# Two-layer token-routing kernel: shared rows added to the output by accumulating transfers, the route mask on ScalarE, raw route weights, traces summed in pairs

## The reference, cut to what matters

```
# conditioning of one sequence (D = 8 decay rates)
ctx    = ema(x, tau_ctx)
gated  = x * sigmoid([x, ctx] @ Wg.T + bg)
mod    = 0.5 + sigmoid(gelu(x @ Wn1.T + bn1) @ Wn2.T + bn2)        # one column for each d
traces = [ema(gated * mod[:, d], tau_raws[d]) for d in range(8)]
temporal = sum_d softmax(blend)[d] * traces[d]
out    = (gelu(x @ Wsoma.T + bsoma) * sigmoid(temporal @ Wtemp.T + btemp)) @ Wout.T
z      = (out - mean) / sqrt(var + 1e-5) * gamma + beta
# expert layer over all 4096 tokens (64 experts, 8 for each token, at most 128 tokens for each expert)
w      = top8(softmax(z @ router.T)); w = w / sum(w)
routed = sum over the 8 experts of  w_e * ((silu(z @ Wgate_e) * (z @ Wup_e)) @ Wdown_e)
shared = (silu(z @ gate) * (z @ up)) @ ws_down
x      = x + routed + shared
```

## Time and profile before

| | |
|---|---|
| median of 3 runs | 1121.03 us (1117.95 to 1122.76) |
| profiled execution, its own time | 1116.69 us |
| its span, from the first to the last instruction | 1114.9 us |
| busy share of the span | PE 86%, DVE 67%, POOL 60%, ACT 41% |
| granted TensorE clock, mean | 0.929 of full |

### The profile page before, as it was taken

How to read it: one execution, slowest core, us unless ns; L and a number is a source line. 1 busy time by engine, 2 the same in 40 slices (tenths; PEclk the granted TensorE clock), 3 DMA queues, 4 the chain that set the end, 5 groups by cost and what they waited for, 6 DMA issues and landing times.

```text
span 1114.9 us, 14811 instructions
## 1 busy us (share of the span) xinstructions
PE 954.6 (86%) x4524; PEld 668.5 (60%) x4524; DVE 743.1 (67%) x1522; ACT 461.2 (41%) x835; POOL 664.1 (60%) x496
## 2 busy tenths in 40 slices
PE   4968999999999999987379899988586899999960
PEld 2533698899989998863144555544353565556640
DVE  3648566667666766524779999999955786777620
ACT  1330444554455545533455665666421232222320
POOL 2113444555455544407999999999931477777870
PEclk9989999999999999988689999999887799999995
DMA  5869234444354432223212752335168599997557
GB/s 174 281 231 352 58 76 118 90 87 99 76 122 90 92 88 39 30 85 76 96 66 70 240 157 86 91 118 182 44 229 274 143 270 256 257 262 150 91 75 157
DMA packets 89782, 155.46 MB, mean 139 GB/s; under 512 B 12072, under 2 KB 70128, under 8 KB 86576
## 3 DMA queue, kind: packets, MB, share of 16 engines
q1 hardware_dynamic: 48112, 91.27, 25.2%
q0 software_dynamic: 25104, 39.86, 20.6%
q10 hardware_dynamic: 16496, 23.49, 6.2%
HBM read 119.56 MB, written 43.42 MB: 146 GB/s over the span
## 4 chain that ended last, share of the span: by engine, by line
POOL 13%; PE 10%; issue 10%; DMA 9%; DVE 4%; ACT 2%; POOLq 2%; DVEq 1%; ACTq 0%; SPq 0%
DMA odd_rows<-ys,slots 5%; POOL wide L635 4%; PE bank L1662 4%; POOL wide L643 3%; DMA xg<-z_rows,slots 2%; POOL xg L721 2%; POOL out L728 2%; POOL odd_rows L728 2%; DVE wide L1271 1%; PE bank L1739 1%; PE bank L1729 1%; PE bank L1722 1%; ACT zrow L945 1%; DMA z_rows<-zrow 1%; ACT wide L895 1%
## 5 line engine op out<-in xcount | busy, mean ns | idle before, releaser
L635 POOL TENSOR_TENSOR wide<-wide 128x1024 f32<-128x1024 f32 x64 | 156.6, 2461 | 30.8 <-issue 30.6
L1271 DVE TENSOR_TENSOR_SCAN wide<-bank,wide 128x512 f32<-128x512 f32 x128 | 149.3, 1209 | 22.8 <-POOL wide L635 22.6
L871 ACT ACTIVATE h_raw<-bank,b 128x512 f32<-128x512 f32 x128 | 88.1, 689 | 168.1 <-PE bank L1635 165.7
L1208 DVE TENSOR_TENSOR h_lo<-h_raw,h_hi 128x512 fp32r<-128x512 f32 x128 | 87.3, 692 | 91.8 <-ACT h_hi L875 91.8
L1650 PE MATMUL bank<-w_hi,h_hi 128*128 128x256 f32 x512 | 144.4, 282 | 0.1
L1650 PE MATMUL bank<-w_lo,h_hi 128*128 128x256 f32 x512 | 142.1, 278 | 0.0
L1650 PE MATMUL bank<-w_hi,h_lo 128*128 128x256 f32 x512 | 142.0, 277 | 0.0
L609 POOL DMA_INDIRECT x_rows<-ob,put x64 | 110.3, 1723 | 28.3 <-issue 16.0
L643 POOL TENSOR_TENSOR wide<-wide 128x1024 f32<-128x1024 f32 x46 | 108.5, 2359 | 11.9 <-issue 8.1
L895 ACT ACTIVATE wide<-wide,blend 128x512 f32<-128x512 f32 x128 | 84.2, 715 | 59.3 <-POOL wide L635 55.5
L1635 PE MATMUL bank<-ex_hi,w_hi 128*128 128x512 f32 x256 | 99.5, 389 | 2.4 <-issue 2.4
(11 more groups left out here) (239 smaller groups left out, 2041.3 us busy)
## 6 DMA issues: line engine op xcount, KB each, us to landing
wide<-in_mwp SPq DMA_DIRECT2D x40, 512.0 KB, 4.5
wide<-m_rows SPq DMA_DIRECT2D x16, 1024.0 KB, 4.9
w1s<-in_fW SPq DMA_DIRECT2D x8, 1024.0 KB, 5.4
w2s<-in_fW SPq DMA_DIRECT2D x8, 1024.0 KB, 5.3
own<-in_mwp SPq DMA_DIRECT2D x15, 512.0 KB, 4.4
z_rows<-zrow SPq DMA_DIRECT2D x8, 640.0 KB, 7.4
head<-in_mwp SPq DMA_DIRECT2D x9, 512.0 KB, 4.5
xT<-in_xT ACTq DMA_DIRECT2D x8, 512.0 KB, 4.2
```

The costliest lines, as they stand in the source:

```text
L635: G.tensor_tensor(drive[n % DRIVES], gb[d % 2], md[d // HD][:, d % HD, :].unsqueeze(1).to_broadcast([P, CT, S]), ALU.mult).then_inc(c_u, 1)
L871: A.activation(h1_raw[f % 4][:, :], bank[:, 2 + f % 4, :], ACT.Gelu_apprx_tanh, bias=b1_0[:, bass.ds(e, 1), f]).then_inc(b_h, 1)
L1208: V.tensor_tensor(h1_lo[:, f, :], h1_raw[f % 4][:, :], h1_hi[:, f, :].bitcast(F32), ALU.subtract).then_inc(b_lo, 1)
L1271: o = V.tensor_tensor_scan(dst[:, c, :], decay[:, d:d + 1].to_broadcast([P, S]), drive[(D * b + d) % DRIVES][:, c, :], 0.0, ALU.mult, ALU.add)
```

## The change

Five edits, all from the conditioning on:

- The base of the result is built in `out` itself: x is copied there, layer 0 adds its rows there, and the conditioning loads its sequences from there. `x1_rows`, `row_in`, `row_store` and `finish` are gone. ACT halves the shared rows from PSUM into `ost` (`share_out`), and POOL issues a transfer that adds `ost` to `out` (`rows_add`).
- The 0/1 mask of sequences 0 to 6 is made by ACT in two instructions, Sign and Relu, straight into `mask_all` (`chosen_out`). The last sequence keeps the comparison on DVE, writing into `mask_all`.
- `zrow` holds the raw products of exponential and mask, and the inverse sum in column 320 (rows are 324 numbers long, 320 before); the expert stage multiplies the two single columns.
- Traces 3 and 4, and traces 5 and 6, are added to one another by DVE (`pair_traces`); POOL adds five sums a sequence (d = 1, 2, 4, 6, 7), DVE adds no single trace to `acc` except the last two of the last sequence.
- The two preparations for the power in `rstd_of` are ACT's (`moments`).

```diff
+        PAIRED = (4, 6)
+        SUMS = tuple(d for d in range(1, D) if d + 1 not in PAIRED)
...
 POOL
             def rstd_of(q):
-                pool.wait_ge(c_mv, level(q))
+                pool.wait_ge(c_mw, level(q))
                 pool.wait_ge(c_no, level(q - 1, TT))
-                G.tensor_scalar(veps1[:, :], mv1[:, :, 1], 4 * EPS, None, ALU.add)
-                G.tensor_scalar(shift1[:, :], mv1[:, :, 0], -1.0, None, ALU.mult)
-                pool.drain()
                 G.tensor_tensor(rstd1[:, :], veps1[:, :], mhalf[:, :], ALU.pow)
...
+            def rows_add(q):
+                pool.wait_ge(c_fin, level(q))
+                pool.dma_start(out[q * S:(q + 1) * S, :].rearrange("(t p) c -> p t c", p=P), ost[:, :, :],
+                               accum_op=ALU.add).then_inc(c_ost, 16)
...
             for e in range(ROWS):
                 e_gather(e)
 
-            pool.wait_ge(c_ost, level(B - 1, 16))
+            rows_add(B - 1)
+            wait_moved(pool, c_ost, B - 1, 16)
...
 ACT
+            def moments(q):
+                act.wait_ge(c_mv, level(q))
+                act.wait_ge(c_no, level(q - 1, TT))
+                A.activation(veps1[:, :], mv1[:, :, 1], ACT.Copy, bias=4 * EPS)
+                A.activation(shift1[:, :], mv1[:, :, 0], ACT.Copy, scale=-1.0).then_inc(c_mw, 1)
...
+            def chosen_out(q):
+                act.wait_ge(c_top, level(q))
+                A.activation(rep[:, :, :], rep[:, :, :], ACT.Sign, bias=far[:, :], scale=-1.0)
+                act.drain()
+                A.activation(mask_all[:, :, q * TT:(q + 1) * TT].rearrange("p e t -> p t e"), rep[:, :, :], ACT.Relu).then_inc(c_ma, 1)
...
+            def share_out(q):
+                act.wait_ge(c_dm, level(q))
+                wait_moved(act, c_ost, q - 1, 16)
+                A.activation(ost[:, :, :], rows4(4), ACT.Copy, scale=0.5).then_inc(c_fin, 1)
...
 DVE
+            def pair_traces(b, d):
+                n = (D - 1) * b + d - 1
+                dve.drain()
+                V.tensor_tensor(trace[n % TRACES], trace[n % TRACES], trace[(n - 1) % TRACES], ALU.add).then_inc(c_pair, 1)
+                dve.drain()
...
             def route_weights(q):
                 dve.wait_ge(c_ex, level(q))
                 dve.wait_ge(c_zst, level(q - 1, 16))
-                V.tensor_tensor(mask[:, :, :], mask[:, :, :], ex[:, :, :], ALU.mult)
+                if q < B - 1:
+                    dve.wait_ge(c_ma, level(q))
+                V.tensor_tensor(zrow[:, :, H:H + E1], ex[:, :, :], chosen(q), ALU.mult)
                 dve.drain()
-                V.tensor_reduce(wsum[:, :], mask[:, :, :], AX.X, ALU.add)
+                V.tensor_reduce(wsum[:, :], zrow[:, :, H:H + E1], AX.X, ALU.add)
                 dve.drain()
-                V.reciprocal(wsum[:, :], wsum[:, :])
-                dve.drain()
-                V.tensor_tensor(zrow[:, :, H:ZW], mask[:, :, :], wsum[:, :].unsqueeze(2).to_broadcast([P, TT, E1]),
-                                ALU.mult).then_inc(c_zr, 1)
+                V.reciprocal(zrow[:, :, H + E1], wsum[:, :]).then_inc(c_zr, 1)
-
-            def finish(q):
-                dve.wait_ge(c_dm, level(q))
-                dve.wait_ge(c_xr, level(q, 16))
-                dve.wait_ge(c_ost, level(q - 1, 16))
-                V.scalar_tensor_tensor(ost[:, :, :], rows4(4), 0.5, xr[:, :, :], ALU.mult, ALU.add).then_inc(c_fin, 1)
```

More of the change, by code:

```diff
@@ L222, in build @@
         neg = sb("neg", [P, TT, E1])
-        mask = sb("mask", [P, TT, E1])
+        far = sb("far", [P, 1])
         ex = sb("ex", [P, TT, E1])
@@ L418, in c_load @@
                 sp.wait_ge(c_Tm, level(n - 2))
-                sp.dma_start(x1t[n % 2], x1_rows[n * S:(n + 1) * S, :].rearrange("(t p) c -> p t c", p=P)).then_inc(c_in[n % 2], 16)
+                sp.dma_start(x1t[n % 2], out[n * S:(n + 1) * S, :].rearrange("(t p) c -> p t c", p=P)).then_inc(c_in[n % 2], 16)
             def e_load(e):
@@ L608, in b_put_rows @@
                 p = r & 1
-                G.indirect_dma_start(x1_rows[:, :], bass.IndirectOffsetOnAxis(ap=put[p][:, j:j + 1], axis=0),
+                G.indirect_dma_start(out[:, :], bass.IndirectOffsetOnAxis(ap=put[p][:, j:j + 1], axis=0),
                                      ob[p][:, j, :], None, compute_op=ALU.add).then_inc(b_put[p], 16)
@@ L663, in step @@
                     drive_of(b - 1, 7)
-                if on(b - 1):
-                    add_trace(b - 1, 5)
                 if ahead(b):
                     drive_of(b, 0)
+                if on(b - 3):
+                    rows_add(b - 3)
                 if ahead(b):
@@ L798, in _ @@
             a_store(B - 1)
-            act.dma_start(x1_rows.rearrange("(a r) c -> a (r c)", a=P), x_rows.rearrange("(a r) c -> a (r c)", a=P)).then_inc(x1_set, 16)
+            act.dma_start(out[0:TOK, :].rearrange("(a r) c -> a (r c)", a=P), x_rows.rearrange("(a r) c -> a (r c)", a=P)).then_inc(x1_set, 16)
             act.wait_ge(zeros_set, 1)
@@ L976, in step @@
                     shared_out(B - 2)
+                    moments(B - 1)
                     normalise(B - 1)
+                    share_out(B - 2)
                     return
@@ L1011, in step @@
                     weighted(b, 7)
+                if on(b - 1):
+                    moments(b - 1)
                 if ahead(b + 1):
                     wg_out(b + 1)
+                if on(b - 2):
+                    share_out(b - 2)
                 if on(b - 1):
@@ L1025, in last_step @@
                 shared_out(B - 1)
+                share_out(B - 1)
             def front_only():
@@ L1267, in scan_unit @@
                     n = (D - 1) * b + d - 1
-                    dve.wait_ge(c_add, level(n - TRACES))
+                    old, of = divmod(n - TRACES, D - 1)
+                    if of + 1 in SUMS and old >= 0:
+                        dve.wait_ge(c_add, added(old, of + 1))
                     dst = trace[n % TRACES]
@@ L1275, in add_trace @@
             def add_trace(b, d):
-                dve.wait_ge(c_scan, level(D * b + d))
+                if d in PAIRED:
+                    dve.wait_ge(c_pair, level(len(PAIRED) * b + PAIRED.index(d)))
+                else:
+                    dve.wait_ge(c_scan, level(D * b + d))
                 if d > 1:
-                    dve.wait_ge(c_add, added(b, d - 1))
+                    dve.wait_ge(c_add, added(b, SUMS[SUMS.index(d) - 1]))
                 dve.drain()
                 V.tensor_tensor(acc[b % 2][:, :, :], acc[b % 2][:, :, :], trace[((D - 1) * b + d - 1) % TRACES], ALU.add).then_inc(c_add, 1)
+            def pair_traces(b, d):
[3 more added lines that the diff above has]
+                dve.drain()
             def ctx_scan(n, held=decay):
@@ L1328, in pick @@
                     to_exponents()
+                dve.wait_ge(c_ma, level(min(q - 1, B - 2)))
                 for j in range(TT):
-                    V.match_replace(rep[:, j, :], top8[:, j, :], lgp[:, j, :], -3.0e38)
-                dve.drain()
-                V.tensor_tensor(mask[:, :, :], rep[:, :, :], lgp, ALU.not_equal).then_inc(c_top, 1)
-                dve.drain()
-                V.tensor_copy(mask_all[:, :, q * TT:(q + 1) * TT].rearrange("p e t -> p t e"), mask[:, :, :])
+                    o = V.match_replace(rep[:, j, :], top8[:, j, :], lgp[:, j, :], -3.0e38)
+                if q < B - 1:
+                    o.then_inc(c_top, 1)
+                else:
+                    dve.drain()
+                    V.tensor_tensor(chosen(q), rep[:, :, :], lgp, ALU.not_equal).then_inc(c_top, 1)
                 if q == B - 1:
@@ L1419, in drain_share @@
                 stats(B - 1)
-                finish(B - 2)
             def last_share():
@@ L1431, in last_share @@
                 prep(1, 0)
-                finish(B - 1)
                 prep(1, 1)
@@ L1475, in step @@
                     scan_unit(b, 6)
-                if on(b - 2):
-                    finish(b - 2)
+                if on(b):
+                    pair_traces(b, 6)
                 if on(b):
```

47 lines of the change are left out of this document (23 added, 24 removed).

## The result

The changed kernel takes 1148.58 us in the median of 4 runs (1148.37 to 1150.08), beside 1119.49 us (1117.80 to 1122.76) for the kernel before on the same chip. The ratio is 1.0259, 95% interval 1.0230 to 1.0288: 29 us slower, where 4.4 were forecast. The profiled execution took 1150.08 us, its span is 1148.3 us. Against the profiled execution before (1116.69), 33.4 us longer, it is 3.1 us ahead at the first `z_in`, 26.9 behind at the last, 29.7 behind at gather 0 and 33.3 behind at the final transfer: nearly all of the loss arises in the steps of the conditioning.

The account below looks back on a forecast made before the run. POOL paced the kernel before; after, PE's 35.1 plus 3.0 of wait gives 38.1 a step. Terms -1.3 + 4.0 + 0.2 - 1.0 + 2.5 = +4.4 on the 1121.03 median: 1125.4 us, range 1116 to 1138.

Parts of the forecast that it names:

- the one on `temp_in`: Conditioning step: POOL's last sum ready 12.8 us after the normalisation, PE at `temp_in` after 13.2, so in time by 0.4.
- Rival 3: POOL's issue of `rows_add` is dear: at 6.9 us instead of 1.2 near 1157, at 3 us near 1133; chance 0.09.
- POOL sets the pace before: Conditioning of the kernel before: POOL's drives, additions and root, 37.8 less overlaps, make up the whole 37.3 us step.
- rival 1: Conditioning: POOL stays the pace and its relief shows, -5 to -8 us, near 1114; chance 0.12.
- POOL's step 36.5: POOL in the conditioning: 37.3 less removed work, plus the pair-sum wait and the `rows_add` issue, gives 36.5 us.
- ACT's additions are no load: ACT in the conditioning: moments, Sign, Relu and halving add 2.5 us, and 26.3 of a step is no load.
- DVE's step 37.2: DVE in the conditioning: 33.7 us plus 3.5 for three operations waiting for POOL, 37.2 a step.
- rival 2: Conditioning: DVE becomes the pace through waits for POOL, step 40.8, +16 us, near 1141, or near 1131; chance 0.15.
- `share_out`, +4.0: ACT's halving ahead of the normalisation: PE's wait ahead of `z_in` becomes 3.0 us in five steps, 15.0 against 11.03.
- Start -1.3: First two conditioning steps, without `share_out`: POOL is the pace and sheds an addition, 1.3 us less.
- last router -1.0: Last router: DVE's final product goes and the z store shares queues with no 512 KB load, 1.0 us less.
- Head of the expert stage +2.5: POOL waits for the last `rows_add` landing ahead of gather 6; scatter 0 5.3 late, partly absorbed: +2.5 us, +1 to +6.

Follow-up runs that it names:

- e1: Changed kernel without POOL's drain ahead of addition 6, the first behind `rows_add`; 1135.02 us, ratio 1.0128 to the kernel before.
- e5: Changed kernel without POOL's drains ahead of additions 6 and 7; 1127.03 us, ratio 1.0043 to the kernel before.
- e9: Changed kernel with all drains, `rows_add` issued directly behind the root, ahead of drives 7, 0 and 1; 1134.40 us, ratio 1.0147.
- g1: Kernel before with one edit: SP issues the z store ahead of the modulation load; 1116.48 us, ratio 0.9962.
- e8: Changed kernel with shared rows loaded by SP, added by DVE, stored by SP as before, no `rows_add` or `share_out`; 1123.65 us, ratio 1.0012.
- e11: e8 with the old trace sums back, six additions on POOL and addition 4 on DVE; 1125.09 us, ratio 1.0063.
- e12: e11 without any drain ahead of POOL's additions; 1120.97 us, ratio 1.0006 to the kernel before.
- f4: f1 with pair sums in place of the old sums; 1110.32 us, ratio 0.9897 to the kernel before.
- f1: e12 with SP issuing the z store ahead of the modulation load; 1104.80 us, ratio 0.9856 to the kernel before.
- g2: f3 with `share_out` back ahead of the normalisation; 1120.07 us, ratio 0.9999 to the kernel before.
- f3: Changed kernel without drains ahead of POOL's additions, `share_out` behind the normalisation, `zrow` doubled, last `rows_add` issued early; 1117.66 us, ratio 0.9968.
- e10: e5 with the last `rows_add` issued ahead of the waits for the z store and of gathers 0 to 5; 1125.12 us, ratio 1.0048.
- e3: Changed kernel with `zrow` doubled, so the normalisation no longer waits for the previous sequence's z store; 1149.36 us, ratio 1.0263.

## Why the prediction was wrong

The step that failed is the one on `temp_in`: "1.3 + 4.9 + 1.5 + 5.1 = 12.8. It does, by 0.4". The issue was sized right (forecast 1.2, measured 1.33). The two additions behind it were priced with the idle time of the earlier trace rows, 0.2, which is that of a drain with no transfer of POOL's under way. Here the drain lasts until the landing: the idle time ahead of addition 6 is 2.2 to 2.8 us, and 8.7 in the first step, whose transfer is issued among five 512 KB loads of expert weights. Ahead of `temp_in` PE then waits 7.9, 1.9, 0.7, 0.8 and 3.6 us, and leaving out both drains is worth 21.6 of the 29 us. e1, e5 and e9 show it three ways. The landing was priced in the expert stage, where the kernel waits for it in so many words, and not in the step, where it waits by a drain. Rival 3 had the place right (POOL's last sum late to `temp_in`), and the time fell between its two prices (1133 and 1157), but it named the issue as the cause.

- *POOL sets the pace before.* Half right: POOL's work alone gives the 37.3, as g1 shows. But the landing of the z store ended within a microsecond of `shift_b`. So POOL's relief had nothing to give by itself (e8, e11, e12), and rival 1 of the prediction, which let it show, missed that too. The two numbers that show it were in the trace: the store's issue, and the gap of 0.47 us where a normalisation that waits only for `shift_b` follows at once.
- *POOL's step 36.5.* Its waits were not in the sum. It now waits 1.9 to 2.2 for pair 4 and 2.8 to 3.7 ahead of drive 0: the addition that was taken out had covered ACT's normalising and scaling. The prediction expected "1 to 2" there and cost it at nothing. f4 against f1 prices the pair sums at +5.
- *ACT's additions are no load.* True of its busy time, not of its order: the mask stands ahead of the sending of the modulation, and so ahead of the z store (see e12). The prediction had no term for it; argued from rows, not isolated.
- *DVE's step 37.2.* The pair sums took 1.29 on average, the product 1.88, where 0.42 is the bare time of such a product, so of the three waits for POOL one came in full and the two of the pair sums hardly at all. DVE was not the bound; rival 2 did not occur.
- *`share_out`, +4.0.* The wait is right to a few hundredths (3.0 forecast, 2.94 measured once the z store is out of the way); in the time it is some 2 to 4 us (g2 against f3, intervals overlapping). In the changed kernel the z store added 0.5 to 2.4 on top.
- *Start -1.3, last router -1.0.* The first `z_in` came 3.1 earlier, but the second step was 2.4 longer (40.0 us against 37.6). From the last `z_in` to gather 0 it was 2.9 longer, not 1.0 shorter: the z store took 13.4 from issue to gather 0, against 10.6. The runs with old rows show 14.1 (e8) and 13.7 (e11) there, so it isn't `rows_add`; why is open. No run shows the half microseconds that the prediction took for these two terms.
- *Head of the expert stage +2.5.* Gather 6 waited 5.64 for the landing and was followed by the first scatter, 26.9 behind gather 0 in place of 21.2, that is 5.7 late where 5.3 were forecast. At the final transfer 3.6 were left, inside the range of +1 to +6. e10, without this wait, was no faster by the ratios, so its worth in the time is not shown.

The rows of gather 6 and the first scatter, which answer to the earlier trace rows:

```profile
910.93 1.07 POOL L716 DMA_INDIRECT xg<-z_rows,slots  x1 [5.64 <-DMA out<-ost]
...
913.60 1.64 POOL L723 DMA_INDIRECT out<-ys,slots  x1 [0.30 <-issue]
```

## What to carry to other kernels

Whoever moves a transfer onto an engine's own queue should look for the next drain on that engine and read the landing, not the issue, as its price; here the additions are already ordered by semaphores, and the drain ahead of them could go. Where an instruction waits for several semaphores, compare its start with the end of each, for the one the profile names may be only the last but one: a gap of half a microsecond in the kernel before was a second limit that ate every gain of the first. The order in which one engine issues transfers is part of such a chain: a store that somebody waits for should not stand behind a load that itself waits. Large loads issued just ahead of a store that somebody waits for cost that store its turn.

## What the runs showed of the hardware

- A drain on POOL lasts until an accumulating DMA that POOL issued has landed (8.68 us of idle time with a landing of 12.3; 2.70 with 6.3; 0.25 where three drives had covered it; none ahead of additions 6 and 7 in e5, which have no drain).
- An accumulating transfer of 512 KB in rows of 1 KB, issued by POOL, took 5.7 to 12.5 us from issue to landing, 6.3 in the median, beside 3.7 for the plain store of the same bytes issued by SP; 11.7 to 12.5 where loads of expert weights were issued around it. The estimate of 3.2 worked out from the Trainium skill ("DMA: Bandwidth & Descriptors", section on the anatomy of a DMA on the GpSimd path) is about half of what was measured.
- A drive that runs while POOL's transfer is being issued takes 2.85 to 2.91 us instead of 2.35.
- The same z store landed in 7.8 us (median) behind a 1 MB load, in 4.4 ahead of it; in the kernel before 7.4, and 3.7 with the swap alone (g1).
- Matmuls behind an idle stretch of PE: the eight on `wsoma` took 3.60 us where PE had waited 1.2 us or less ahead of `z_in` (f1, granted clock 1.00 of full), 4.4 to 5.7 where it had waited 3.4 or more (e12, 0.59 of full from 616.2 to 623.4 us). The wait alone does not decide it: in e3 the transposes behind a wait of 2.94 us took 1.09 us, in g2 behind the same wait 1.97.
